# Mixture-of-experts output: weighted rows and an adding scatter in place of two rows per token and a combine

## The chip, the core and the metric

The kernel runs on one core of one Trainium2 chip. The core has TensorE (PE), VectorE (DVE), ScalarE (ACT), GpSimd (POOL) and SyncE (SP), each with its own instruction queue, and 16 DMA engines that all queues share. The metric is the device time of one execution in microseconds, lower is better.

## What is computed

The input x is 16 x 256 x 16 x 16 (batch, nodes, features, time). A spatio-temporal attention block with a Chebyshev graph convolution is added to x; then a group norm of the result goes through eight experts, of which each token uses two. A token is one of the 16 x 256 = 4,096 positions (batch, feature and time), with 256 channels. The change lies in the second part alone:

```
probs = softmax(x @ gate_w.T)                   # per token, 8 experts
rw, sel = top_k(probs, 2);  rw = rw / sum(rw)
combine = sum(one_hot(sel, 8) * rw)             # per token and expert
out = 0
for e in range(8):
    h = gelu(x @ w1[e].T) * (x @ w3[e].T)
    out = out + combine[:, e:e+1] * (h @ w2[e].T)
result = residual + transpose(out)              # back to channels first
```

## The kernel before

The work runs in stages: loads and attention statistics (to about 120 us of the profiled execution), the main phase over 16 batches with graph convolution, norms and routing (to about 435 us), the expert stage (444 to 671 us), and the last stage (671 to 717 us). The order on each engine is written out by hand, with semaphores between engines; there is no scheduler.

Routing (route_b and route_c on DVE) finds for each token its two experts, their weights r2[:, 3] / sum and r2[:, 4] / sum, and a slot for each in the DRAM tensor xrows, where the tokens of one expert stand together. POOL scatters the token's row there twice. A row is 256 channels and two numbers: the token's index (column N) and its first expert (column N + 1). Unused places of an expert's last tile are filled with rows whose index lies out of range.

The expert stage walks over RUN = 71 tiles of 128 rows. For each tile t, SP loads the rows (L312) into xt, of which there are four; PE transposes them (L605); DVE copies them out of PSUM (copy_x, L1400) and computes the row in yrows to which each result goes (L1403, L1406): the token's index, plus 4,096 if the tile's expert is not the token's first. PE does the first product (L618), ACT the gelu (L819), DVE the gate (L1411), PE a transposition (L626) and the second product (L633), with ACT's copy (L830) between these. ACT copies the result out of PSUM into one of four buffers yo (copy_y, L825), and POOL casts the destinations to integers (L936) and scatters 128 rows of 1 KB into yrows (put_rows, L940). So yrows has 8,192 rows, two for each token, each written once. POOL raises c_out, for which copy_y waits, after it has seen the scatter of three tiles earlier landed.

On PE the order within a tile is: transpose_rows of tile t + 3, down of t, turn_hidden of t + 1, up of t + 3.

The last stage goes over the 16 batches. SP loads both rows of each token (L332, L333; two transfers of 256 KB into one of four buffers yy), ACT multiplies the first with its weight (weigh_first, L854, two operations), DVE multiplies the second and adds (combine, L1435, two operations), PE transposes (L667, four), DVE adds the residual xs (L1444) into one of two buffers oo, and ACT issues the store (L859). These buffers, xt and yo among them, all lie over the tensor xT, which is the name that the profile shows.

Of the kernel before, what the change touches and what calls it, by code (L numbers as in the profile page):

```python
# [21 lines left out]
P = 128  # L22
# [13 lines left out]
ROW = N + 2  # L36
# [83 lines left out]
def build(nc, x, consts, small, cheb, vst, bst, w13t, w2t, xrows, yrows, out):  # L120
    with ExitStack() as ctx:
# [70 lines left out]
        wts = sb("wts", [B, 2, TT])  # L192
# [34 lines left out]
        dn = over_xT(2, 4, 1)  # L227
        used[0] = 0
        yy = over_xT(4, 2, TT, N)
        ym = over_xT(4, TT, N)  # L230
        ys = over_xT(2, TT, N)
        oo = over_xT(2, C, FT)
# [24 lines left out]
        d_ym = sem("d_ym"); c_ld = [sem(f"c_ld{i}") for i in range(SLOTS)]; c_tr = sem("c_tr"); c_xc = sem("c_xc"); c_up = sem("c_up")  # L257
# [4 lines left out]
        d_ld = [sem(f"d_ld{i}") for i in range(4)]; d_in = sem("d_in"); d_s = sem("d_s"); d_tr = sem("d_tr")  # L262
        d_o = sem("d_o"); d_st = [sem("d_st0"), sem("d_st1")]
# [8 lines left out]
        y_v = yrows[0:2 * TOKENS, :].rearrange("(w b k p) n -> p w b k n", w=2, b=B, k=TT)  # L272
# [10 lines left out]
        def _(sp):  # L283
# [16 lines left out]
            sp.wait_ge(fill_ready, 1)  # L300
            sp.dma_start(xrows[E * CAP:E * CAP + P, :], fill[:]).then_inc(fill_done, 16)
# [29 lines left out]
            def load_d(b, q):  # L331
                sp.dma_start(yy[:, q, 0], y_v[:, 0, b]).then_inc(d_ld[q], 16)  # L332
                sp.dma_start(yy[:, q, 1], y_v[:, 1, b]).then_inc(d_ld[q], 16)  # L333

            def landed(q, pairs):

                sp.wait_ge(d_ld[q], 32 * pairs)
                sp.sem_inc(d_in, 1)

            for q in range(4):  # L340
                load_d(q, q)
            landed(0, 1)
            landed(1, 1)
            with sp.Fori(0, B // 4 - 1) as i:
                for q in range(4):
                    landed((q + 2) % 4, i + (1 if q < 2 else 2))
                    sp.wait_ge(d_s, 4 * i + (q + 1 + START))
                    load_d(4 * i + (q + 4), q)
            landed(2, B // 4)
            landed(3, B // 4)  # L350
# [3 lines left out]
        def _(pe):  # L354
# [305 lines left out]
            with pe.Fori(0, B // 2) as i:  # L660
                for q in range(2):
                    b = 2 * i + q
                    pe.wait_ge(d_s, b + (1 + START))
                    pe.wait_ge(d_o, b + START - 1)
                    for c in range(C):
                        for k in range(TT):
                            last = nc.tensor.transpose(bank[6 + q][:, c * FT + k * P:c * FT + (k + 1) * P],  # L667
                                                       ys[:, q, k, c * P:(c + 1) * P], ident)
                    last.then_inc(d_tr, 1)
# [3 lines left out]
        def _(act):  # L673
# [148 lines left out]
            def copy_y(t, q):  # L822
                act.wait_ge(c_dn, t + (1 + START))
                act.wait_ge(c_out, t + 1)
                nc.scalar.copy(yo[:, t % 4], bank[4 + q][:, 0:N]).then_inc(c_y, 1)  # L825
# [23 lines left out]
            def weigh_first(b):  # L849
                act.wait_ge(d_in, b + 1)  # L850
                if not isinstance(b, int):
                    act.wait_ge(d_s, b + (START - 3))
                for k in range(TT):
                    ins = nc.scalar.mul(ym[:, b % 4, k], yy[:, b % 4, 0, k], wts[:, b, 0, k:k + 1])  # L854
                ins.then_inc(d_ym, 1)

            def store(b, q):
                act.wait_ge(d_o, b + (1 + START))
                act.dma_start(out_v[:, b], oo[:, q]).then_inc(d_st[q], 16)  # L859

            weigh_first(0)
            weigh_first(1)
            with act.Fori(0, B // 2 - 1) as i:
                for q in range(2):
                    weigh_first(2 * i + (q + 2))
                    store(2 * i + q, q)
            store(B - 2, 0)
            store(B - 1, 1)
            for q in range(2):
                act.wait_ge(d_st[q], 16 * (B // 2))  # L870
# [3 lines left out]
        def _(pool):  # L874
# [57 lines left out]
            def put_rows(t, q):  # L932

                pool.wait_ge(c_de, t + 1)
                pool.nop(nofuse=True)
                nc.gpsimd.tensor_copy(dest[:, q], dn[:, 1, q]).then_inc(c_di, 1)  # L936
                pool.wait_ge(c_y, t + (1 + START))
                pool.wait_ge(c_di, t + (1 + 4))
                pool.nop(nofuse=True)
                pool.indirect_dma_start(yrows, bass.IndirectOffsetOnAxis(ap=dest[:, q], axis=0),  # L940
                                        yo[:, q], None, bounds_check=2 * TOKENS - 1, oob_is_err=False
                                        ).then_inc(c_st[q], 16)

            for q in range(3):
                put_rows(q, q)
            with pool.Fori(0, (RUN - 3) // 4) as i:
                for q in range(4):
                    put_rows(4 * i + (q + 3), (q + 3) % 4)
# [7 lines left out]
        def _(dve):  # L956
# [296 lines left out]
            def route_b(b, p):  # L1253
# [22 lines left out]
                wb = wts[:, b]  # L1276
                V.tensor_tensor(wb[:, 0], r2[:, 3], r2[:, 8], ALU.mult)
                yield from step.then(V.tensor_tensor(wb[:, 1], r2[:, 4], r2[:, 8], ALU.mult))
# [248 lines left out]
```

## Time and profile before

| | us |
|---|---|
| median of 3 runs | 720.68 (719.37 to 721.49) |
| the profiled execution: its time | 719.21 |
| the profiled execution: its span, first to last instruction | 717.4 |
| expert stage, first to last scatter of results (71) | 458.0 to 668.4 |
| last stage, first load to the end | 670.7 to 717.4 |
| PE busy in the span, mean granted clock | 570.1, 0.883 |

The span is that of the instructions in one profiled execution; its time has 1.8 us around it. "Granted clock" is TensorE's clock as a share of 2.4 GHz; 0.50 is 1.2 GHz. A row of the timeline gives the start, the duration, and in brackets how long the engine was idle and what released it. A DMA issue counts on the engine that issues it; "to landing" is the time from the start of the issue until the data has arrived.

### The profile page before, as it was taken

What the parts mean: (1) busy time and instruction counts of PE and PEld (TensorE: products, weight loads), DVE (VectorE), ACT (ScalarE), POOL (GpSimd) and SP (SyncE); (2) the same over time, 40 slices, a digit from 0 to 9 for tenths busy, and PEclk for the clock granted to TensorE, in tenths of its full rate; (3) what the DMA queues carried; (4) which work ended last, traced back from release to release, by engine and by line L of the source; (5) the groups of instructions that cost most, each with busy time, mean ns of one, the idle gap of its engine ahead of it and who ended that gap; (6) DMA issues with size and microseconds to landing.
All of it is one profiled execution on the core that took longest, in us unless ns stands there. A gap on an engine that the chain in (4) does not pass through costs nothing. (4 is left out here: it accounts for less than half of the span.)

```text
span 717.4 us, 12846 instructions
## 1 busy us (share of the span) xinstructions
PE 570.1 (79%) x2508; PEld 372.1 (52%) x2509; DVE 426.7 (59%) x1891; ACT 250.4 (35%) x623; POOL 207.0 (29%) x265
## 2 busy tenths in 40 slices
PE   0566649999999999999997332999999999999344
PEld 0333325776666666666675110566666666666122
DVE  6755432687898888888888764333333333333255
ACT  0312214444444444444442210233333333333232
POOL 1000000111444444343444432133333333434100
PEclk9866668999999999999999655999999999999555
DMA  8910000000000000000000015122222222221497
GB/s 269 374 58 0 0 1 0 1 1 0 31 31 30 29 29 29 29 29 29 29 30 30 30 59 125 61 82 88 81 83 88 83 87 84 85 86 48 145 314 244
DMA packets 36247, 52.69 MB, mean 73 GB/s; under 512 B 4605, under 2 KB 31360, under 8 KB 35968
## 3 DMA queue, kind: packets, MB, share of 16 engines
q1 hardware_dynamic: 24816, 30.86, 13.7%
q0 software_dynamic: 6480, 16.85, 6.4%
q10 hardware_dynamic: 4928, 4.72, 2.0%
q8 instruction: 8, 0.13, 0.1%
q14 instruction: 15, 0.12, 0.1%
HBM read 30.19 MB, written 23.14 MB: 74 GB/s over the span
## 5 line engine op out<-in xcount | busy, mean ns | idle before, releaser
L618 PE MATMUL bank<-w,xT 128*128 x284 | 135.8, 601 | 2.1 <-DVE xT L1400 2.1
L1400 DVE COPY xT<-bank 128x256 f32<-128x256 f32 x71 | 30.2, 425 | 144.1 <-PE bank L605 144.1
L940 POOL DMA_INDIRECT yrows<-xT,dest x71 | 69.4, 977 | 140.5 <-ACT xT L825 136.3
L496 PE MATMUL bank<-work 128*128 128x256 f32 x384 | 94.8, 390 | 0.0
L909 POOL DMA_INDIRECT xrows<-xtok,slot x64 | 64.2, 1003 | 82.3 <-DVEq L1296 67.7
L897 POOL TENSOR_TENSOR yg<-work,sml 128x512 f32<-128x512 f32 x16 | 17.9, 1120 | 224.5 <-DVE work L1206 224.5
L496 PEld LDWEIGHTS bank<-work 128*128 128x128 f32 x384 | 71.5, 193 | 9.4 <-issue 0.8
L633 PE MATMUL bank<-w,xT 128*128 x284 | 74.2, 384 | 1.8 <-ACT xT L830 1.8
L618 PEld LDWEIGHTS bank<-w,xT 128*128 128x128 f32 x284 | 48.8, 192 | 37.6 <-issue 37.6
L819 ACT ACTIVATE xT<-bank 128x256 f32<-128x256 f32 x71 | 27.2, 383 | 95.3 <-PE bank L618 95.3
L633 PEld LDWEIGHTS bank<-w,xT 128*128 128x128 f32 x284 | 49.0, 192 | 6.5 <-issue 2.7
L825 ACT COPY xT<-bank 128x256 f32 (+1 forms) x71 | 26.4, 372 | 60.9 <-PE bank L633 60.9
L605 PEld LDWEIGHTS bank<-cst,xT 128*128 128x128 f32 x142 | 20.2, 143 | 52.7 <-issue 37.5
L487 PE MATMUL bank<-thetabd,xTb 128*128 128x384 f32 x128 | 46.6, 487 | 0.0
L773 ACT ACTIVATE xn<-xs,gr 128x256 f32 (+1 forms) x32 | 17.5, 592 | 71.1 <-DVE gr L1233 71.1
L667 PE MATMUL bank<-cst,xT 128*128 128x128 f32 x64 | 17.8, 433 | 29.1 <-DVE xT L1435 29.1
L605 PE MATMUL bank<-cst,xT 128*128 128x128 f32 x142 | 27.7, 277 | 15.1 <-DMA xT<-xrows 15.1
L467 PE MATMUL bank<-sg,vs 128*128 128x256 f32 x128 | 33.4, 406 | 2.5 <-ACT sg L735 1.4
L1155 DVE TENSOR_TENSOR work<-bank,chebs 128x768 f32<-128x768 f32 x32 | 30.1, 947 | 5.1 <-PE bank L478 5.1
L1411 DVE TENSOR_TENSOR xT<-bank,xT 128x256 f32<-128x256 f32 x71 | 30.2, 425 | 2.1 <-ACT xT L819 2.1
L755 ACT COPY work<-bank 128x384 f32<-128x384 f32 x64 | 28.9, 472 | 7.2 <-PE bank L487 6.5
L532 PE MATMUL bank<-xn,sml 128*8 128x256 f32 x64 | 19.0, 426 | 14.4 <-ACT xn L773 14.4
(204 smaller groups left out, 1060.6 us busy)
## 6 DMA issues: line engine op xcount, KB each, us to landing
xT<-xrows SPq DMA_DIRECT2D x71, 129.0 KB, 2.1
xT<-yrows SPq DMA_DIRECT2D x32, 256.0 KB, 4.0
xs<-x_in SPq DMA_DIRECT2D x4, 1024.0 KB, 6.6
w<-w13t_in SPq DMA_DIRECT2D x1, 4096.0 KB, 15.4
out<-xT ACTq DMA_DIRECT2D x16, 256.0 KB, 3.8
w<-w2t_in SPq DMA_DIRECT2D x1, 2048.0 KB, 19.8
yrows<-xT,dest POOLq DMA_INDIRECT x71, 2.4
xrows<-xtok,slot POOLq DMA_INDIRECT x64, 2.6
```

The source lines that it names most:

```text
L467: last = mm(bank[1][:, c * N:(c + 1) * N], vs[:, j, c * P:(c + 1) * P], sg[:, p, j], start=(j == 0), stop=(j == C - 1))
L487: mm(bank[4 + h][:, 0:K * P], xTb[:, p, h, c * P:(c + 1) * P], thetabd[:].rearrange("p k t o -> p (k t o)"), start=True, stop=True).then_i ...
L496: last = mm(bank[6][:, h * N:(h + 1) * N], z[:, p, c, k, h], A[:, p, c, k], start=(c == 0 and k == 0), stop=(c == C - 1 and k == K - 1))
L605: last = nc.tensor.transpose(bank[k % 2][:, c * P:(c + 1) * P], xt[:, k % SLOTS, c * P:(c + 1) * P], ident)
L618: last = mm(bank[2 + q][:, :], xc[:, q, c], w13[:, e, c].rearrange("p w n -> p (w n)"), start=(c == 0), stop=(c == C - 1))
L633: last = mm(bank[4 + q][:, 0:N], hT[:, q, f], w2[:, e, f], start=(f == 0), stop=(f == C - 1))
L755: nc.scalar.copy(z[:, p, c, :, h], bank[4 + h][:, 0:K * P].rearrange("p (k o) -> p k o", k=K)).then_inc(s["b_zc"], 1)
L909: pool.indirect_dma_start(xrows, bass.IndirectOffsetOnAxis(ap=slot[:, q, w, k:k + 1], axis=0), xtok[:, q, k], None).then_inc(sc_done[q], 16)
L940: pool.indirect_dma_start(yrows, bass.IndirectOffsetOnAxis(ap=dest[:, q], axis=0), yo[:, q], None, bounds_check=2 * TOKENS - 1, oob_is_err ...
L1155: ins = V.tensor_tensor(A[:, p, c], p3, chebs[:, c], ALU.mult)
L1400: V.tensor_copy(xc[:, q].rearrange("p c k -> p (c k)"), bank[q][:, 0:C * P]).then_inc(c_xc, 1)
L1411: V.tensor_tensor(hh[:, q].rearrange("p f k -> p (f k)"), bank[2 + q][:, C * P:2 * C * P], gl[:, q].rearrange("p f k -> p (f k)"), ALU.mul ...
```

## The change

The kernel gives each row four extra numbers in place of two: the two weights go with it (columns N + 2 and N + 3), so xrows has rows of 260 numbers. In the expert stage DVE computes the row's weight for the tile's expert as the sum of two products with a comparison (four operations where two stood), and copy_y multiplies with it while it copies. The destination is the token's index itself. yrows holds one row per token; the scatter adds to it, in DRAM. Since two scatters may add to one row, each waits until the one before it has landed. SP zeroes yrows ahead of that, with 16 transfers behind the weights' load, and POOL waits for them before the first scatter. In the last stage SP loads one row per token, six batches ahead; weigh_first and combine are gone, PE transposes straight from yy, and there are three buffers oo. The loops of that stage are written out in place of loops on the engines.

```diff
--- before.py
+++ after.py
@@ -33,7 +33,7 @@
 TT = FT // P
 TOKENS = B * FT
 CAP = TOKENS + P
-ROW = N + 2
+ROW = N + 4
 TILES = 2 * TOKENS // P + E
 EPS = 1e-5
 BITS = E.bit_length() - 1
...
@@ -224,12 +223,10 @@
         hh = over_xT(2, C, P)
         hT = over_xT(2, C, P)
         yo = over_xT(4, N)
-        dn = over_xT(2, 4, 1)
+        dn = over_xT(4, 4, 1)
         used[0] = 0
-        yy = over_xT(4, 2, TT, N)
-        ym = over_xT(4, TT, N)
-        ys = over_xT(2, TT, N)
-        oo = over_xT(2, C, FT)
+        yy = over_xT(6, TT, N)
+        oo = over_xT(3, C, FT)
 
 
         ld_c = sem("ld_c"); ld_w = sem("ld_w"); ld_m = sem("ld_m")
...
@@ -269,7 +266,7 @@
 
         x_v = x.rearrange("b (c p) f t -> p b c (f t)", p=P)
         out_v = out.rearrange("b (c p) f t -> p b c (f t)", p=P)
-        y_v = yrows[0:2 * TOKENS, :].rearrange("(w b k p) n -> p w b k n", w=2, b=B, k=TT)
+        y_v = yrows[0:TOKENS, :].rearrange("(b k p) n -> p b k n", b=B, k=TT)
 
         def fill_behind(eng, experts):
             for e in experts:
@@ -298,6 +295,9 @@
                 sp.dma_start(dst[:], src).then_inc(ld_m, 16)
 
             sp.wait_ge(fill_ready, 1)
+            zeros = fill[:, 0:N].rearrange("p (u n) -> p u n", u=1).to_broadcast([P, TT, N])
+            for b in range(B):
+                sp.dma_start(y_v[:, b], zeros).then_inc(z_done, 16)
             sp.dma_start(xrows[E * CAP:E * CAP + P, :], fill[:]).then_inc(fill_done, 16)
             sp.wait_ge(fill_rows, 1)
             fill_behind(sp, range(E // 2))
@@ -328,26 +328,14 @@
 
             for q in range(4):
                 sp.wait_ge(c_st[q], 16 * ((RUN + 3 - q) // 4))
-            def load_d(b, q):
-                sp.dma_start(yy[:, q, 0], y_v[:, 0, b]).then_inc(d_ld[q], 16)
-                sp.dma_start(yy[:, q, 1], y_v[:, 1, b]).then_inc(d_ld[q], 16)
-
-            def landed(q, pairs):
-
-                sp.wait_ge(d_ld[q], 32 * pairs)
-                sp.sem_inc(d_in, 1)
-
-            for q in range(4):
-                load_d(q, q)
-            landed(0, 1)
-            landed(1, 1)
-            with sp.Fori(0, B // 4 - 1) as i:
-                for q in range(4):
-                    landed((q + 2) % 4, i + (1 if q < 2 else 2))
-                    sp.wait_ge(d_s, 4 * i + (q + 1 + START))
-                    load_d(4 * i + (q + 4), q)
-            landed(2, B // 4)
-            landed(3, B // 4)
+            def load_d(b):
+
+                if b >= 6:
+                    sp.wait_ge(d_tr, b - 5)
+                sp.dma_start(yy[:, b % 6], y_v[:, b]).then_inc(d_ld[b % 6], 16)
+
+            for b in range(B):
+                load_d(b)
 
 
         @block.tensor
@@ -657,16 +645,15 @@
                     turn_hidden(t + 1, (t + 1) % 2)
 
 
-            with pe.Fori(0, B // 2) as i:
-                for q in range(2):
-                    b = 2 * i + q
-                    pe.wait_ge(d_s, b + (1 + START))
-                    pe.wait_ge(d_o, b + START - 1)
-                    for c in range(C):
-                        for k in range(TT):
-                            last = nc.tensor.transpose(bank[6 + q][:, c * FT + k * P:c * FT + (k + 1) * P],
-                                                       ys[:, q, k, c * P:(c + 1) * P], ident)
-                    last.then_inc(d_tr, 1)
+            for b in range(B):
+                pe.wait_ge(d_ld[b % 6], 16 * (b // 6 + 1))
+                if b >= 2:
+                    pe.wait_ge(d_o, b - 1)
+                for c in range(C):
+                    for k in range(TT):
+                        last = nc.tensor.transpose(bank[6 + b % 2][:, c * FT + k * P:c * FT + (k + 1) * P],
+                                                   yy[:, b % 6, k, c * P:(c + 1) * P], ident)
+                last.then_inc(d_tr, 1)
 
 
         @block.scalar
@@ -822,7 +809,8 @@
             def copy_y(t, q):
                 act.wait_ge(c_dn, t + (1 + START))
                 act.wait_ge(c_out, t + 1)
-                nc.scalar.copy(yo[:, t % 4], bank[4 + q][:, 0:N]).then_inc(c_y, 1)
+                act.wait_ge(c_de, t + 1)
+                nc.scalar.mul(yo[:, t % 4], bank[4 + q][:, 0:N], dn[:, 3, t % 4]).then_inc(c_y, 1)
 
             def copy_hidden(t, q):
                 act.wait_ge(c_ht, t + (1 + START))
@@ -846,28 +834,11 @@
             copy_y(RUN - 1, (RUN - 1) % 2)
 
 
-            def weigh_first(b):
-                act.wait_ge(d_in, b + 1)
-                if not isinstance(b, int):
-                    act.wait_ge(d_s, b + (START - 3))
-                for k in range(TT):
-                    ins = nc.scalar.mul(ym[:, b % 4, k], yy[:, b % 4, 0, k], wts[:, b, 0, k:k + 1])
-                ins.then_inc(d_ym, 1)
-
-            def store(b, q):
-                act.wait_ge(d_o, b + (1 + START))
-                act.dma_start(out_v[:, b], oo[:, q]).then_inc(d_st[q], 16)
-
-            weigh_first(0)
-            weigh_first(1)
-            with act.Fori(0, B // 2 - 1) as i:
-                for q in range(2):
-                    weigh_first(2 * i + (q + 2))
-                    store(2 * i + q, q)
-            store(B - 2, 0)
-            store(B - 1, 1)
-            for q in range(2):
-                act.wait_ge(d_st[q], 16 * (B // 2))
+            for b in range(B):
+                act.wait_ge(d_o, b + 1)
+                act.dma_start(out_v[:, b], oo[:, b % 3]).then_inc(d_st[b % 3], 16)
+            for q in range(3):
+                act.wait_ge(d_st[q], 16 * ((B + 2 - q) // 3))
 
 
         @block.gpsimd
@@ -929,23 +900,27 @@
 
             pool.sem_inc(c_di, 4)
 
-            def put_rows(t, q):
+            def put_rows(t, q, landed):
 
                 pool.wait_ge(c_de, t + 1)
                 pool.nop(nofuse=True)
                 nc.gpsimd.tensor_copy(dest[:, q], dn[:, 1, q]).then_inc(c_di, 1)
                 pool.wait_ge(c_y, t + (1 + START))
                 pool.wait_ge(c_di, t + (1 + 4))
+
+                if landed is not None:
+                    pool.wait_ge(c_st[(q - 1) % 4], landed)
                 pool.nop(nofuse=True)
                 pool.indirect_dma_start(yrows, bass.IndirectOffsetOnAxis(ap=dest[:, q], axis=0),
-                                        yo[:, q], None, bounds_check=2 * TOKENS - 1, oob_is_err=False
-                                        ).then_inc(c_st[q], 16)
-
+                                        yo[:, q], None, bounds_check=TOKENS - 1, oob_is_err=False,
+                                        compute_op=ALU.add).then_inc(c_st[q], 16)
+
+            pool.wait_ge(z_done, 16 * B)
             for q in range(3):
-                put_rows(q, q)
+                put_rows(q, q, 16 if q else None)
             with pool.Fori(0, (RUN - 3) // 4) as i:
                 for q in range(4):
-                    put_rows(4 * i + (q + 3), (q + 3) % 4)
+                    put_rows(4 * i + (q + 3), (q + 3) % 4, 16 * i + 16 * ((q + 2) // 4 + 1))
                     pool.wait_ge(c_st[q], 16 * (i + 1))
                     pool.sem_inc(c_out, 1)
             for q in range(4):
@@ -1273,9 +1248,8 @@
                 V.tensor_scalar(xtok[:, p, :, N + 1], r2[:, 5], -1.0, float(E), ALU.mult, ALU.add)
                 yield from step.then(V.tensor_tensor(r2[:, 7], r2[:, 3], r2[:, 4], ALU.add))
                 yield from step.then(V.reciprocal(r2[:, 8], r2[:, 7]))
-                wb = wts[:, b]
-                V.tensor_tensor(wb[:, 0], r2[:, 3], r2[:, 8], ALU.mult)
-                yield from step.then(V.tensor_tensor(wb[:, 1], r2[:, 4], r2[:, 8], ALU.mult))
+                V.tensor_tensor(xtok[:, p, :, N + 2], r2[:, 3], r2[:, 8], ALU.mult)
+                yield from step.then(V.tensor_tensor(xtok[:, p, :, N + 3], r2[:, 4], r2[:, 8], ALU.mult))
                 step.close()
 
             def route_c(b, p):
@@ -1400,10 +1374,14 @@
                 V.tensor_copy(xc[:, q].rearrange("p c k -> p (c k)"), bank[q][:, 0:C * P]).then_inc(c_xc, 1)
 
                 dve.wait_ge(c_di, t + 1)
-                V.tensor_scalar(dn[:, 0, m], xt[:, m, N + 1:N + 2], tb3[:, 0, bass.ds(t, 1)], float(TOKENS),
-                                ALU.not_equal, ALU.mult).then_inc(c_dd, 1)
+                if not isinstance(t, int) or t >= 4:
+                    dve.wait_ge(c_y, t + START - 3)
+                e = tb3[:, 0, bass.ds(t, 1)]
+                V.tensor_scalar(dn[:, 0, m], xt[:, m, N + 1:N + 2], e, xt[:, m, N + 2:N + 3], ALU.is_equal, ALU.mult)
+                V.tensor_scalar(dn[:, 2, m], xt[:, m, N + 1:N + 2], e, xt[:, m, N + 3:N + 4], ALU.not_equal, ALU.mult)
+                V.tensor_copy(dn[:, 1, m], xt[:, m, N:N + 1]).then_inc(c_dd, 1)
                 dve.wait_ge(c_dd, t + 1)
-                V.tensor_tensor(dn[:, 1, m], dn[:, 0, m], xt[:, m, N:N + 1], ALU.add).then_inc(c_de, 1)
+                V.tensor_tensor(dn[:, 3, m], dn[:, 0, m], dn[:, 2, m], ALU.add).then_inc(c_de, 1)
 
             def gate(t, q):
                 dve.wait_ge(c_gl, t + 1)
@@ -1424,37 +1402,12 @@
             gate(RUN - 1, (RUN - 1) % 2)
 
 
-            dve.sem_inc(d_o, START)
-            dve.sem_inc(d_s, START)
-
-            def combine(b, q):
-
-                dve.wait_ge(d_in, b + 1)
-                dve.wait_ge(d_ym, b + 1)
-                for k in range(TT):
-                    ins = V.scalar_tensor_tensor(out=ys[:, q, k], in0=yy[:, b % 4, 1, k], scalar=wts[:, b, 1, k:k + 1],
-                                                 in1=ym[:, b % 4, k], op0=ALU.mult, op1=ALU.add)
-                ins.then_inc(d_s, 1)
-
-            def residual(b, q, stored):
-
+            for b in range(B):
                 dve.wait_ge(d_tr, b + 1)
-                if stored is not None:
-                    dve.wait_ge(d_st[q], stored)
-                V.tensor_tensor(oo[:, q].rearrange("p c n -> p (c n)"), bank[6 + q][:, :],
+                if b >= 3:
+                    dve.wait_ge(d_st[b % 3], 16 * (b // 3))
+                V.tensor_tensor(oo[:, b % 3].rearrange("p c n -> p (c n)"), bank[6 + b % 2][:, :],
                                 xs[:, b].rearrange("p c n -> p (c n)"), ALU.add).then_inc(d_o, 1)
-
-            combine(0, 0)
-            for b in range(2):
-                combine(b + 1, 1 - b)
-                residual(b, b, None)
-            with dve.Fori(0, B // 2 - 2) as i:
-                for q in range(2):
-                    combine(2 * i + (q + 3), 1 - q)
-                    residual(2 * i + (q + 2), q, 16 * (i + 1))
-            combine(B - 1, 1)
-            residual(B - 2, 0, 16 * (B // 2 - 1))
-            residual(B - 1, 1, 16 * (B // 2 - 1))
 
 
 def constants():
```

On POOL, one tile of the loop of the expert stage and the start of the next, before the change (CAST is the cast of destinations, the DMA is the scatter; line numbers are those of the kernel before):

```order
L936 CAST dest<-xT 128x1 [waits c_de]
L937 REGISTER_ALU
L938 REGISTER_ALU [waits c_y]
L940 DMA yrows<-xT,dest 8320x256 [waits c_di]
L949 ISA
L934 REGISTER_ALU [waits c_st0]
L936 CAST dest<-xT 128x1 [waits c_de]
```

The same place after the change (lines are those of the changed kernel):

```order
L907 CAST dest<-xT 128x1 [waits c_de]
L908 REGISTER_ALU
L909 REGISTER_ALU [waits c_y]
L912 ISA [waits c_di]
L914 DMA yrows<-xT,dest 8320x256 [waits c_st2]
L924 ISA
L905 REGISTER_ALU [waits c_st0]
L907 CAST dest<-xT 128x1 [waits c_de]
```

The scatter now has the wait for c_st2 in front of it, which is the landing of the scatter just before; the cast of the next tile stays behind the scatter, as it was.

On DVE, one tile of the loop of the expert stage before the change (copy_x, the destination, gate):

```order
L1400 COPY xT<-bank 128x256 [waits c_up,c_tr]
L1403 ISA [waits c_di]
L1403 TENSOR_SCALAR xT<-xT,tb 128x1
L1406 TENSOR_TENSOR xT<-xT 128x1 [waits c_dd]
L1411 TENSOR_TENSOR xT<-bank,xT 128x256 [waits c_ht,c_gl]
```

The same tile after the change:

```order
L1374 COPY xT<-bank 128x256 [waits c_up,c_tr]
L1380 ISA [waits c_y,c_di]
L1380 TENSOR_SCALAR xT<-xT,tb 128x1
L1381 TENSOR_SCALAR xT<-xT,tb 128x1
L1382 COPY xT<-xT 128x1
L1384 TENSOR_TENSOR xT<-xT 128x1 [waits c_dd]
L1389 TENSOR_TENSOR xT<-bank,xT 128x256 [waits c_ht,c_gl]
```

Two small operations more stand between copy_x and gate, and the first of them also waits for c_y, ACT's copy_y of four tiles before.

## Rows read from the trace of the kernel before

**Rows 1.** Page, table 1: busy us (share of the span) and instructions of TensorE
```profile
...
PE 570.1 (79%) x2508; PEld 372.1 (52%) x2509; DVE 426.7 (59%) x1891; ACT 250.4 (35%) x623; POOL 207.0 (29%) x265
...
```

**Rows 2.** Windows: before the main phase, steady expert stage, last stage
```profile
core 0: us, PE busy (x) PEld busy (x) DVE busy (x) ACT busy (x) POOL busy (x), PEclk, DMA share, GB/s
40.00:60.00 20.00, 12.86 (x50) 6.48 (x50) 11.79 (x50) 4.42 (x9) 0.00 (x0) 0.67 0.00 0
465.00:620.00 155.00, 155.00 (x618) 95.72 (x617) 54.28 (x208) 52.69 (x154) 59.99 (x103) 1.00 0.27 85
671.00:717.40 46.40, 17.78 (x64) 11.44 (x64) 24.14 (x48) 14.52 (x32) 0.00 (x0) 0.50 0.84 271
...
```

**Rows 3.** Timeline, one tile: start us, us, engine line op tiles [idle before <-releaser]
```profile
...
540.23 0.42 DVE L1400 COPY xT<-bank 128x256 f32<-128x256 f32 x1 [1.94 <-PE bank L605]
...
540.57 0.20 DVE L1403 TENSOR_SCALAR xT<-xT,tb 128x1 f32<-128x1 f32 x1
...
540.80 0.16 DVE L1406 TENSOR_TENSOR xT<-xT 128x1 f32<-128x1 f32 x1
540.88 0.42 DVE L1411 TENSOR_TENSOR xT<-bank,xT 128x256 f32<-128x256 f32 x1
...
541.11 1.88 PE L618 MATMUL bank<-w,xT 128*128 x4
541.29 0.37 ACT L825 COPY xT<-bank 128x256 f32 x1 [0.83 <-PE bank L633]
...
542.58 0.98 POOL L940 DMA_INDIRECT yrows<-xT,dest  x1 [1.92 <-ACT xT L825]
...
```

**Rows 4.** Tile dest: duration ns, starts of the scatters, and time to landing
```profile
...
L940 POOL DMA_INDIRECT yrows<-xT,dest x71: 976/976/1002, 458.0 to 668.4; - x71
...
DMA to landing us min/median/max: 2.1/2.4/2.8
```

**Rows 5.** Timeline, scatters of routed rows of one batch in the main phase
```profile
...
308.62 0.17 DVE L1293 CAST slot<-slotf 128x4 int32<-128x4 f32 x1
...
309.66 1.01 POOL L909 DMA_INDIRECT xrows<-xtok,slot  x1 [4.36 <-DVEq L1296]
310.97 0.96 POOL L909 DMA_INDIRECT xrows<-xtok,slot  x1 [0.30 <-issue]
...
```

**Rows 6.** DMA, 465 to 620 us: queue share; issues with us to landing
```profile
...
q0 software_dynamic: 2490, 6.49, 10.4%
...
xT<-xrows SPq DMA_DIRECT2D x51, 129.0 KB, 2.1
...
```

**Rows 7.** Timeline: last scatter, first load of the last stage, last residual
```profile
...
668.43 0.98 POOL L940 DMA_INDIRECT yrows<-xT,dest  x1 [2.06 <-ACT xT L825]
670.67 0.40 SPq L332 DMA_DIRECT2D xT<-yrows  x1
...
714.04 0.69 DVE L1444 TENSOR_TENSOR xT<-bank,xs 128x512 f32<-128x512 f32 x1 [0.68 <-PE bank L667]
```

**Rows 8.** Chain that ended last, in order of time, in the last stage
```profile
...
679.47 4.68 DMA out<-xT
...
685.16 4.50 DMA out<-xT
...
```

**Rows 9.** DMA, 671 to 717.4 us
```profile
...
DMA packets 13057, 12.59 MB, mean 271 GB/s; under 512 B 768, under 2 KB 13056, under 8 KB 13056
...
xT<-yrows SPq DMA_DIRECT2D x32, 256.0 KB, 4.0
out<-xT ACTq DMA_DIRECT2D x16, 256.0 KB, 3.8
```

**Rows 10.** Timeline: the first tile's product L618
```profile
...
445.37 3.77 PE L618 MATMUL bank<-w,xT 128*128 x4 [0.70 <-DVE xT L1400]
...
```

**Rows 11.** Timeline of SP: its last issues ahead of 432 us
```profile
...
20.00 0.53 SPq L298 DMA_DIRECT2D w<-w2t_in  x1
20.57 0.43 SPq L301 DMA_DIRECT2D xrows<-fill  x1
...
```

More of the change, by code:

```diff
@@ L191, in build @@
         r2 = sb("r2", [10, TT])
-        wts = sb("wts", [B, 2, TT])
         cnt = sb("cnt", [E])
@@ L255, in build @@
         v_tb = sem("v_tb"); tables = sem("tables"); fill_rows = sem("fill_rows"); fill_ready = sem("fill_ready"); fill_done = sem("fill_done")
-        d_ym = sem("d_ym"); c_ld = [sem(f"c_ld{i}") for i in range(SLOTS)]; c_tr = sem("c_tr"); c_xc = sem("c_xc"); c_up = sem("c_up")
+        z_done = sem("z_done"); c_ld = [sem(f"c_ld{i}") for i in range(SLOTS)]; c_tr = sem("c_tr"); c_xc = sem("c_xc"); c_up = sem("c_up")
         c_gl = sem("c_gl"); c_h = sem("c_h"); c_ht = sem("c_ht"); c_hc = sem("c_hc"); c_dn = sem("c_dn"); c_y = sem("c_y"); c_dd = sem("c_dd")
@@ L260, in build @@
         c_st = [sem(f"c_st{i}") for i in range(4)]; c_out = sem("c_out")
-        d_ld = [sem(f"d_ld{i}") for i in range(4)]; d_in = sem("d_in"); d_s = sem("d_s"); d_tr = sem("d_tr")
-        d_o = sem("d_o"); d_st = [sem("d_st0"), sem("d_st1")]
+        d_ld = [sem(f"d_ld{i}") for i in range(6)]; d_tr = sem("d_tr")
+        d_o = sem("d_o"); d_st = [sem(f"d_st{i}") for i in range(3)]
         cs = lambda a, n: cst[:, a:a + n]
```

## The prediction

> **What bounds the kernel now.** I read the page first: TensorE is busy 570.1 of 717.4 us, 79% of the span [rows 1]. That share is an average, so I cut the span by stages. From 465 to 620 us, the steady part of the expert stage, PE is busy in all of 155.00 us at a granted clock of 1.00, while DVE has 54, ACT 53 and POOL 60 us; the 16 DMA engines are 27% busy. In the last stage, from 671 to 717.4 us, the shares turn round: PE 17.8 of 46.4 us, DMA 84% busy [rows 2]. So there are two stages here that the change touches, one set by PE and one by DMA.
>
> The pace of the expert stage is best read from its last engine. The 71 scatters of result rows (L940) start between 458.0 and 668.4 us [rows 4], so one tile takes 210.4 / 70 = 3.006 us. I then followed one tile through the engines: copy_x, two small DVE operations, gate, the first product (L618), copy_y, and the scatter [rows 3]. The point to see is the distance from copy_y to the scatter: the copy ends at 541.29 + 0.37 = 541.66 us and the scatter starts at 542.58, although POOL was idle for 1.92 us and nothing else was missing. The 16 groups of routing scatters show this too: the slots are written at 308.79 us, the first scatter starts at 309.66 (0.87 later), and the next, which waits for nothing, 1.31 after that, 0.30 after the end of the first [rows 5]. So 0.9 us pass between the release of a scatter and its start as recorded. They hide behind a preceding scatter only if the next may be released before that one is done. In the kernel before nobody waits for this: four result buffers give each scatter several tiles of time.
>
> **The added wait.** A scatter now waits until its predecessor has landed. On POOL it stands directly ahead of the DMA; the cast for the same tile stands ahead of the wait, but the cast of the next tile is queued behind the scatter. What follows is a ring of steps, none of which can overlap: release, 0.92 us to the start, landing, release of the next. Landing is 2.4 us from the start in the median (2.1 at the least, 2.8 at most) [rows 4], which already has the 0.98 us of descriptor writing in it. The signal itself is quick: the last scatter starts at 668.43 and SP issues the load that waits for it at 670.67, 2.24 later [rows 7]. A ring of plain scatters so takes 0.92 + 2.4 = 3.32 us, 0.31 more than the 3.006 us that PE leaves it. Over 70 intervals that is +22 us before the addition itself costs anything. PE and ACT follow: copy_y of tile t waits for c_out, which POOL raises only after it has issued the scatter of tile t-1, so the banks of the second product come free at the ring's pace.
>
> **The addition.** No row shows an adding scatter. Below, its surcharge on the landing is 0: it writes the same bytes with the same descriptors' targets, and I see no reason for it to be faster than a plain one. Above, I take a whole load in sequence ahead of the write: a tile's 129 KB load lands 2.1 us after its issue [rows 6]. Between them: queue 0 spends 10.4% of 16 engines over 155 us on 51 scatters, 0.32 us for each scatter on each engine [rows 6]. Reading the destination as well makes that 0.64 (+0.3). Descriptors for a second read, if they are written at the rate of the others, add up to half of 0.98 us, part of it under the transfer (+0.3). I choose 0.6, nearer the lower end, since the rows of a scatter can be read ahead of each other. The ring is then 3.92 us, 0.914 above 3.006: 70 x 0.914 = +64 us.
>
> The Trainium skill (Collectives: The Full Stack, Part 3, "Why ReduceScatter is half of AllGather") says that an adding transfer is slower not for the addition but since it reads two sources, both through one ring. By that alone the surcharge would be the 0.3 us of doubled transfer, which is a rival below; no row here shows an addition.
>
> The wait can't be dropped for speed: two tiles of different experts hold the same token, and both would add to one row. The Trainium skill (DMA: Bandwidth & Descriptors, Rules for kernel authors) says so too: an accumulating DMA reads its destination and writes it later, and one that lands in between is lost. No run here shows it, and it changes no number.
>
> **The last stage.** Gone are 16 of 32 loads of 256 KB, ACT's weighing (2 operations) and DVE's combine (2 operations, L1435) for each batch. The chain there runs through stores: 679.47 to 685.16 us from one store to the next in the chain, which is two batches, since residual waits for the store before last out of two buffers; the stores in between land after 4.68 and 4.50 us [rows 8]. Now there are three buffers. Two estimates: (a) 12.59 MB took 84% of 46.4 us, 39 us of full engines, 323 GB/s [rows 2, 9]; 8.39 MB take 26.0, and with the 7.4 us that the engines were not full, 33.4 us. (b) By latency: a period of about 5.2 us over three buffers, 1.75 a batch, 15 x 1.75 = 26, after some 6 us to the first store and ahead of 2.7 us from the last residual's end (714.73) to the end [rows 7]: 35 us. The stage gives back 11 to 13 us; I take 13. PE needs 1.1 us a batch even at its present clock of 0.50 there (17.78 us for 16), and DVE 0.69, so neither replaces DMA.
>
> **What costs nothing.** The 16 stores of zeros (4.2 MB, 13 us at 323 GB/s) are issued on SP after the weights' load at 20.00 us. The only transfer issued behind them until 432 us is the store of fill, and the DMA share from 40 to 60 us is 0.00 [rows 2, 11]. Without that cover they would cost 13 us. On DVE a tile gets two operations more and one other kind: 0.20 + 0.16 become four of about 0.2, +0.4 us. DVE idles 1.94 us ahead of each copy_x, and gate's result of 541.30 us is wanted by PE for the next tile's turn, over 2 us later [rows 3]. DVE's new wait for c_y is for the copy of four tiles back. copy_y changes from a copy to a product with a column, at the same shape. Rows of 260 for 258 numbers add 0.8% to transfers that are hidden. The weights' writes into xtok replace as many into wts, and the scatter of those rows is behind the same semaphore.
>
> **Sum.** The profiled execution took 719.2 us around a span of 717.4. 719.2 + 22 (ring of plain scatters) + 42 (70 x 0.6, the addition) - 13 = 770.2 us. That execution stands 1.5 us below the median of the three runs shown, 720.68; I leave it at 770.
>
> **Rivals.**
> - *The ring is hidden.* If most of the 0.92 us is preparation that POOL's queue does before the wait is fulfilled, the ring is 2.4 to 3.0 us and PE's 3.006 stays the pace: 719.2 - 13 = 706. For it: 0.30 us between neighbouring scatters. Against it: at 309.66 and at 542.58 an idle POOL, its instruction waiting, still took 0.87 and 0.92. It is faster than before if the ring stays under 3.006 + 13/70 = 3.19 us. Chance 0.12.
> - *Only the reads double.* Surcharge 0 to 0.3: ring up to 3.62, 719.2 + 43 - 13 = 749, down to 728. For it: transfers are a small part of the landing. Chance 0.22.
> - *The addition is slow, or PE's clock falls.* Surcharge over 1.1: 70 x 1.42 - 13 + 719.2 = 805 and more; with a full load in sequence (ring 5.42) 875. At a ring of 3.92 PE is busy 77% of the time. Four L618 products took 3.77 us at the lower clock at the stage's start [rows 10] against 1.88 later; if half of the tiles ran so, at 6.0 us each, the mean would be 4.96 and the time 843. Chance 0.18.
> - My forecast, surcharge 0.3 to 1.1, 749 to 805 us: 0.44. A ring within 0.03 us of 3.19, where gain and loss meet: 0.04.
>
> **How the numbers follow.** A measurement here tells 0.3% (2.2 us) from no change. Faster is the first rival, 0.12; same 0.04; slower is the rest, 0.84. The range must take in the second rival's 728 and reach into the third; 722 to 838 leaves out the hidden ring (0.12) and the far end of the slow addition (0.07). The forecast's own range is 749 to 805.
>
> **What would show it.** In the profile after, the scatters' mean interval should be 3.9 us (3.3 if the addition is free), the wait ahead of the scatter should go from copy_y to the scatter before it, PE should show a gap of 0.9 us per tile, and landing should read 3.0 in place of 2.4. The last stage should take 33 us with no SCALAR_TENSOR_TENSOR in it. A mean interval of 3.0 proves the first step wrong; an interval of 3.3 the surcharge alone.

## The result: 814.4 us, 13% slower

The changed kernel takes 814.36 us (813.15 to 816.02, 4 runs) against 720.17 us before in the same job: a ratio of 1.129 [1.127, 1.132]. The forecast had slower at 0.84 and 770 us; the time lies in its range of 722 to 838, in the third rival's part of it, to which I had given 0.18; the central case, 749 to 805 us at 0.44, ends 9 us short of it. The profiled execution has a span of 812.6 us, 95.2 more than before.

**Pace of the expert stage.** The view of the scatters' destinations in the changed kernel, which answers to [rows 4]; the first two columns of a row are line and engine, then duration in ns (min/median/max) and first and last start:

```profile
L907 POOL CAST dest<-xT x71: 183/781/801, 446.4 to 777.6; 128x1 int32<-128x1 f32 x71
L914 POOL DMA_INDIRECT yrows<-xT,dest x71: 1557/1569/1629, 458.8 to 780.1; - x71
its engine sat idle before it (us, times) until:
  DMA yrows<-xT,dest: 183.9, 66
...
DMA to landing us min/median/max: 2.7/3.8/4.3
```

The interval is (780.1 - 458.8) / 70 = 4.590 us, where it was 3.006. POOL now waits for its own last transfer 66 times. Landing takes 3.8 us in place of 2.4, and POOL's own record of a scatter, which I take for the writing of its descriptors, 1.57 in place of 0.98.

One turn of the ring in the timeline, with PE and ACT behind it:

```profile
...
601.94 1.56 POOL L914 DMA_INDIRECT yrows<-xT,dest  x1 [2.94 <-DMA yrows<-xT,dest]
602.07 0.48 ACT L813 ACTIVATE xT<-bank,xT 128x256 f32 x1 [3.70 <-POOLq L925]
...
602.92 0.78 POOL L907 CAST dest<-xT 128x1 int32<-128x1 f32 x1
...
603.14 1.13 PE L621 MATMUL bank<-w,xT 128*128 x4 [1.45 <-issue]
...
606.46 1.57 POOL L914 DMA_INDIRECT yrows<-xT,dest  x1 [2.75 <-DMA yrows<-xT,dest]
```

The order of releases has turned round: in [rows 3] the scatter waited for copy_y; here copy_y (L813) waits 3.70 us for POOL to raise c_out (L925), and PE's second product (L621) starts 1.45 us late behind it. The bracket names no releaser for this one; over the span, the profile puts 61.0 of the 88.1 us that PE idles ahead of L621 down to ACT's L818, which stands behind copy_y on ACT.

**Windows**: the time of zeroing and the steady expert stage. These answer to [rows 2]:

```profile
core 0: us, PE busy (x) PEld busy (x) DVE busy (x) ACT busy (x) POOL busy (x), PEclk, DMA share, GB/s
40.00:60.00 20.00, 12.53 (x49) 6.46 (x50) 12.15 (x52) 3.86 (x8) 0.00 (x0) 0.59 0.56 196
500.00:700.00 200.00, 143.43 (x521) 82.70 (x520) 62.40 (x259) 45.16 (x132) 77.64 (x88) 0.99 0.36 56
...
```

PE is busy in 72% of the time from 500 to 700 us, at a clock of 0.99. (From 740 to 777 us, at the stage's end, the clock is 0.87, with PE busy in 24.0 of 37 us.) The zeros fill a window from 40 to 60 us that was empty.

**The DMA queue of the scatters** from 480 to 700 us (packets, MB, share of 16 engines), which answers to [rows 6]:

```profile
q0 software_dynamic: 6891, 5.95, 24.2%
```

48 scatters start in this window: 144 packets for one, and 0.242 x 220 / 48 = 1.11 us on each DMA engine. Before it was 49 packets and 0.32 us, for the same 0.12 MB.

**The last stage.** The last scatter, the loads behind it, and the first residual, answering to [rows 7]:

```profile
780.09 1.57 POOL L914 DMA_INDIRECT yrows<-xT,dest  x1 [1.75 <-DMA yrows<-xT,dest]
782.96 17.88 SPq L335 DMA_DIRECT2D xT<-yrows  x16
...
787.09 0.69 DVE L1409 TENSOR_TENSOR xT<-bank,xs 128x512 f32<-128x512 f32 x1 [22.03 <-PE bank L654]
...
793.41 0.69 DVE L1409 TENSOR_TENSOR xT<-bank,xs 128x512 f32<-128x512 f32 x1 [0.50 <-DMA out<-xT]
```

From the first load at 782.96 to 812.6 it is 29.6 us, where it was 46.7. From the fourth batch on, the first that needs a buffer again, the residual is held in 10 of 13 batches by a store (the bracket), though there are three buffers. The stage in the window's columns of above:

```profile
783.00:812.60 29.60, 16.74 (x64) 11.83 (x64) 11.05 (x16) 0.00 (x0) 0.00 (x0) 0.56 0.86 283
```

The span's 95.2 us are thus: 70 x (4.590 - 3.006) = +110.9 in the ring, +0.8 until the first scatter, +0.6 from the last one to the first load (2.87 for 2.24 us), -17.1 in the last stage.

### The profile page after: what moved, and what is told of

Read it like the earlier page. It is cut to its first block and busy times, and to the rows that moved or that the text cites. A ratio compares the mean times of both kernels' runs of the same rounds, so it can differ in the third digit from the quotient of the medians.

```text
span 812.6 us, 12753 instructions
## 1 busy us (share of the span) xinstructions
PE 592.2 (73%) x2508; PEld 377.6 (46%) x2509; DVE 441.1 (54%) x2001; ACT 237.0 (29%) x591; POOL 249.4 (31%) x265
## 5 line engine op out<-in xcount | busy, mean ns | idle before, releaser
L914 POOL DMA_INDIRECT yrows<-xT,dest x71 | 111.3, 1568 | 209.7 <-DMA yrows<-xT,dest 183.9
L621 PE MATMUL bank<-w,xT 128*128 x284 | 82.7, 415 | 88.1 <-ACT xT L818 61.0
L606 PE MATMUL bank<-w,xT 128*128 x284 | 138.6, 612 | 2.1 <-DVE xT L1374 2.1
L813 ACT ACTIVATE xT<-bank,xT 128x256 f32 (+1 forms) x71 | 33.8, 476 | 242.7 <-POOLq L925 119.9
L621 PEld LDWEIGHTS bank<-w,xT 128*128 128x128 f32 x284 | 49.7, 195 | 107.6 <-issue 103.6
L1374 DVE COPY xT<-bank 128x256 f32<-128x256 f32 x71 | 30.1, 425 | 114.9 <-PE bank L593 114.9
L1380 DVE TENSOR_SCALAR xT<-xT,tb 128x1 f32<-128x1 f32 x71 | 19.3, 272 | 102.6 <-POOL dest L907 102.6
L606 PEld LDWEIGHTS bank<-w,xT 128*128 128x128 f32 x284 | 50.4, 198 | 39.3 <-issue 39.3
L907 POOL CAST dest<-xT 128x1 int32<-128x1 f32 x71 | 54.8, 772 | 7.3 <-DVE xT L1384 7.3
L593 PE MATMUL bank<-cst,xT 128*128 128x128 f32 x142 | 27.7, 277 | 13.4 <-DMA xT<-xrows 13.4
L1130 DVE TENSOR_TENSOR work<-bank,chebs 128x768 f32<-128x768 f32 x32 | 30.1, 947 | 5.1 <-PE bank L466 5.0
L1389 DVE TENSOR_TENSOR xT<-bank,xT 128x256 f32<-128x256 f32 x71 | 30.1, 425 | 2.9 <-ACT xT L806 2.9
```

The lines of the kernel that those rows point to most:

```text
L593: last = nc.tensor.transpose(bank[k % 2][:, c * P:(c + 1) * P], xt[:, k % SLOTS, c * P:(c + 1) * P], ident)
L606: last = mm(bank[2 + q][:, :], xc[:, q, c], w13[:, e, c].rearrange("p w n -> p (w n)"), start=(c == 0), stop=(c == C - 1))
L621: last = mm(bank[4 + q][:, 0:N], hT[:, q, f], w2[:, e, f], start=(f == 0), stop=(f == C - 1))
L813: nc.scalar.mul(yo[:, t % 4], bank[4 + q][:, 0:N], dn[:, 3, t % 4]).then_inc(c_y, 1)
L1130: ins = V.tensor_tensor(A[:, p, c], p3, chebs[:, c], ALU.mult)
L1374: V.tensor_copy(xc[:, q].rearrange("p c k -> p (c k)"), bank[q][:, 0:C * P]).then_inc(c_xc, 1)
```

## The experiments

My theory: the time is lost in a ring (release, start, landing) that nothing overlaps, and the addition lengthens the landing. The rivals: the wait alone is harmless; adding scatters are a bound in throughput; something else in the changed tile, such as the weighted copy or DVE's operations, sets the pace.

**1. The wait alone.** The kernel before with the wait added:

```diff
                 pool.wait_ge(c_di, t + (1 + 4))
+                if landed is not None:
+                    pool.wait_ge(c_st[(q - 1) % 4], landed)
                 pool.nop(nofuse=True)
...
```

> The kernel before with one thing added: each scatter waits until its predecessor has landed. Scatters stay plain, two rows per token. My theory (a ring of release, start, landing): release to start 0.8 us (as the adding scatters of the changed kernel show it) plus 2.4 us landing gives 3.2 us per filled tile against 3.006, 67 filled tiles: +13 us, about 732 us; with 0.92 us as in the prediction 3.32 and +21, 740 us. Rival (the addition is the whole loss, the wait alone is hidden behind PE): 720 us, interval 3.01.

Measured: 735.36 us against 718.65, ratio 1.025 [1.022, 1.028]. Its scatters, in the same view:

```profile
L942 POOL DMA_INDIRECT yrows<-xT,dest x71: 976/979/1003, 456.7 to 682.8; - x71
...
DMA to landing us min/median/max: 2.1/2.4/2.7
```

The interval is 226.1 / 70 = 3.230 us. A ring of plain scatters is longer than PE's work by 0.22 us: 2.4 of landing and 0.83 from release to start. The rival of a harmless wait is out. Of the 16.7 us measured, 70 x 0.224 = 15.7 are the ring's.

**2. The changed kernel with a plain scatter**, still one at a time:

```diff
-                                        yo[:, q], None, bounds_check=TOKENS - 1, oob_is_err=False,
-                                        compute_op=ALU.add).then_inc(c_st[q], 16)
+                                        yo[:, q], None, bounds_check=TOKENS - 1, oob_is_err=False
+                                        ).then_inc(c_st[q], 16)
```

> The changed kernel with a plain scatter in place of the adding one (this leaves out the sum of the two experts of a token, the later one overwrites); the wait stays. Ring theory: interval 3.2 us as in the run with the wait alone, last stage 29.6 us as in the changed kernel, so 719 + 13 - 17 = 715 us, descriptor writing back at 0.98 us and landing at 2.4. Rival (something else in the changed expert stage, such as the weighted copy or the four DVE operations, holds the pace): interval stays near 4.6, 814 us.

Measured: 720.56 us, ratio 1.003 [1.001, 1.004] (ten runs from 717.8 to 723.9):

```profile
L914 POOL DMA_INDIRECT yrows<-xT,dest x71: 977/979/1002, 458.6 to 690.3; - x71
```

The interval is 231.7 / 70 = 3.31, and descriptor writing is back at 0.98 us. The rival of 4.6 is out: POOL waits for its own last transfer here too (68 times), and not for the weighted copy or DVE's four operations. Taking one argument of one instruction away gives back some 92 us (94.2 above the kernel before in one job, 1.9 in the other). The expectation of 715 us was missed by 5.6, for the interval is 0.08 above run 1: landing is 2.5 in the stage's middle for 2.4, and two scatters land only after 3.3 and 4.0 us. What makes the plain landing longer in the changed kernel stays open.

**3. Adding without the wait**, each tile to rows of its own (not shown: 16 further transfers of zeros for the second half of yrows, and the bound of 2 * TOKENS - 1):

```diff
-                if landed is not None:
-                    pool.wait_ge(c_st[(q - 1) % 4], landed)
...
-                V.tensor_copy(dn[:, 1, m], xt[:, m, N:N + 1]).then_inc(c_dd, 1)
+                V.tensor_scalar(dn[:, 1, m], xt[:, m, N + 1:N + 2], e, float(TOKENS), ALU.not_equal, ALU.mult).then_inc(c_dd, 1)
...
+                V.tensor_tensor(dn[:, 1, m], dn[:, 1, m], xt[:, m, N:N + 1], ALU.add).then_inc(c_de, 1)
```

> Adding scatters without the wait: each tile adds to rows of its own (8192 rows, all zeroed, 32 zero stores), and the last stage still loads one row per token (this leaves out the second expert's part). Latency theory: the addition costs only where it is waited for, POOL needs 1.57 + 0.3 us per scatter and DMA 1.1 us per engine, both under PE's 3.006: interval 3.01, 719 - 17 = 702 us. Rival (the adding scatter is a bound in throughput, on POOL or the DMA engines): interval over 3.2, over 715 us.

Measured: 702.22 us, ratio 0.978 [0.975, 0.981]. The timeline shows a scatter released by the copy again, as 62 of the 71 are:

```profile
559.78 1.56 POOL L915 DMA_INDIRECT yrows<-xT,dest  x1 [1.12 <-ACT xT L816]
```

and in the view of destinations:

```profile
L915 POOL DMA_INDIRECT yrows<-xT,dest x71: 1557/1569/1629, 460.2 to 670.3; - x71
```

First to last start is 210.1 us, interval 3.00. The addition is no bound in throughput at this pace: it costs its latency, and only where that is waited for. The 16.4 us gained are the one-row last stage (30.1 us from its first load to the end).

**4. No rows in the adding scatter**: every destination out of range.

```diff
-                V.tensor_copy(dn[:, 1, m], xt[:, m, N:N + 1]).then_inc(c_dd, 1)
+                V.tensor_scalar(dn[:, 1, m], xt[:, m, N:N + 1], float(TOKENS), None, ALU.add).then_inc(c_dd, 1)
```

> The changed kernel with every destination out of range, so that no row is written (this leaves out the experts' whole result); adding form and wait stay. The last three scatters of the changed kernel, of tiles without tokens, came 3.5 us apart and landed in 2.7. Theory: the rows' transfer is 1.1 us of the ring, so all intervals become 3.5 us and the expert stage 70 x 1.07 = 75 us shorter, near 739 us. Rival (the last scatters are quicker for another reason, such as that the loads of tiles are over): interval 4.4 to 4.6.

Measured in one run: 744.8 us (739 expected), and

```profile
L914 POOL DMA_INDIRECT yrows<-xT,dest x71: 1557/1569/1629, 459.9 to 710.6; - x71
...
DMA to landing us min/median/max: 2.7/2.7/4.1
```

The interval is 3.58 us. So of the filled ring's 4.59, 1.0 is the rows' transfer. The plain scatter's empty tiles land in 2.1 (the least value in [rows 4]), its filled ones in 2.4. The addition's surcharge of 1.4 us on the landing has two parts: 0.6 is there without rows, as much as the writing of descriptors has grown, and 0.8 comes with the rows' transfer.

**5. Half the bytes**: the first 128 of 256 columns of each row (yh is yrows seen as rows of half the length, so the index is doubled).

```diff
-                pool.indirect_dma_start(yrows, bass.IndirectOffsetOnAxis(ap=dest[:, q], axis=0),
-                                        yo[:, q], None, bounds_check=TOKENS - 1, oob_is_err=False,
+                pool.indirect_dma_start(yh, bass.IndirectOffsetOnAxis(ap=dest[:, q], axis=0),
+                                        yo[:, q, 0:N // 2], None, bounds_check=2 * TOKENS - 1, oob_is_err=False,
...
-                V.tensor_copy(dn[:, 1, m], xt[:, m, N:N + 1]).then_inc(c_dd, 1)
+                V.tensor_scalar(dn[:, 1, m], xt[:, m, N:N + 1], 2.0, None, ALU.mult).then_inc(c_dd, 1)
```

> The changed kernel scattering the first 128 of 256 columns of each row alone (this leaves out half of the channels' sum), 512 bytes where 1 KB was; the number of rows and of descriptors is the same. The filled ring of 4.59 us has 1.1 us over the empty one of 3.58. If the transfer goes by bytes the interval becomes 4.1 us, 779 us in all; if by rows it stays at 4.5 to 4.6, 812 us.

Measured in one run: 780.4 us:

```profile
L916 POOL DMA_INDIRECT yrows<-xT,dest x71: 1557/1569/1630, 459.2 to 746.7; - x71
```

The interval is 4.11, landing 3.3. The part of the ring above the empty one goes by bytes: 0.53 us for 1.01, while the rows and their packets (143 for a scatter) are as many as before. The time on each DMA engine follows less closely: 0.173 x 220 / 54 = 0.70 us for 1.11.

**6. Two rings in turn**: even and odd tiles add to different halves of yrows, and each scatter waits for the one two tiles back (not shown: the zeros for both halves, and TOKENS added to the destination for odd tiles).

```diff
-                    pool.wait_ge(c_st[(q - 1) % 4], landed)
+                    pool.wait_ge(c_st[(q - 2) % 4], landed)
```

> The changed kernel with two halves of yrows: even tiles add to one, odd tiles to the other, and a scatter waits for the landing of the scatter two tiles back in place of the one before. The last stage loads the even half alone (this leaves out what the odd tiles added). Theory (the wait costs by latency, 4.59 us for one turn of the ring, now shared by two tiles, 2.3 each): PE's 3.01 us is the pace again, 702 us as in the run without waits. Rival (adding scatters that overlap slow each other, their 1.1 us on each DMA engine and 1.57 us on POOL in a row): interval 3.2 to 3.5, 716 to 737 us.

Measured: 703.64 us, ratio 0.977 [0.972, 0.982]:

```profile
L917 POOL DMA_INDIRECT yrows<-xT,dest x71: 1558/1569/1630, 459.5 to 670.0; - x71
```

The interval is 210.5 / 70 = 3.01, landing still 3.8. A ring of 4.6 us costs nothing if two tiles share it. A whole kernel would have to load both halves again in the last stage, which takes back what the adding scatter was for. There is a cheaper way that no run tried: the tiles come in the order of the experts, and a token's two experts differ, so two tiles of one expert never share a token. Only where the expert changes, at most seven times in 71 tiles, must a scatter wait for those before it. What such a kernel would take is not shown.

**7. Two rows per token, weighted in the copy**, plain scatters, no wait; in the last stage two loads and one addition on DVE for each batch, six pairs of row buffers and four result buffers.

```diff
-        yy = over_xT(6, TT, N)
-        oo = over_xT(3, C, FT)
+        yy = over_xT(6, 2, TT, N)
+        oo = over_xT(4, C, FT)
...
+                V.tensor_tensor(yy[:, b % 6, 0], yy[:, b % 6, 0], yy[:, b % 6, 1], ALU.add).then_inc(d_s, 1)
...
```

> The other half of the change without the adding scatter: rows weighted in copy_y, plain scatters to two rows per token with no wait, and a last stage as in the changed kernel but with two loads of 256 KB per batch, one DVE addition, six buffers for rows and four for results. Theory A (the last stage before was held by store latency over two buffers, DMA engines can move more): 12.59 MB at 350 to 380 GB/s is 33 to 36 us plus 6 of head and tail, 40 to 42 against 46.7 us, so 713 to 716 us (median of before 720). Theory B (DMA was full at 96%): 46 us, no change.

Measured: 710.48 us, ratio 0.987 [0.983, 0.991]; the last stage is 39.6 us in place of 46.7. Theory A held. Since this run changed the weighing and the build of the last stage at once, run 8 parts these two.

**8. The last stage rebuilt, the weighing kept**: the kernel before, unweighted rows, its own weighing in place on ACT and DVE, with the buffers of run 7. The loops are written out too, SP no longer waits for a load to land before it issues a later one, and a row buffer is loaded again once PE, and not DVE, has read it.

```diff
-        yy = over_xT(4, 2, TT, N)
-        ym = over_xT(4, TT, N)
-        ys = over_xT(2, TT, N)
-        oo = over_xT(2, C, FT)
+        yy = over_xT(6, 2, TT, N)
+        oo = over_xT(4, C, FT)
...
```

> The kernel before with the buffers and the written-out order of the two-row run in its last stage (six pairs of row buffers, four result buffers), but with its own weighing on ACT and DVE, in place. Theory A (the gain of that run came from the buffers, the stage being held by stores over two buffers): 40 us for the stage, 711 to 714 us in all, as with weighted rows. Theory B (it came from leaving out ACT's weighing and one of DVE's two operations): 46 us, 719 us.

Measured: 709.52 us, ratio 0.987 [0.983, 0.990], the same as run 7. Its last stage in the window's columns of above:

```profile
672.00:708.70 36.70, 17.85 (x64) 11.46 (x64) 23.85 (x48) 14.52 (x32) 0.00 (x0) 0.50 0.96 324
```

ACT does as much weighing as before and the gain is there all the same. This window starts 3.5 us after the stage's first load; over the whole stage, 668.5 to 708.7 us, the DMA engines are at 92% where they were at 84%. Weighting in the copy gives nothing by itself. Runs 7 and 8 can't be told apart; they are the fastest versions whose edits leave nothing of the output out, 1.3% below the kernel before. Which of the edits to the stage gives the 6.5 us (46.7 to 40.2), no run tells. For the result buffers speak the chain of stores in [rows 8] and run 9. But SP's waits for landings, behind which it issued the later loads in the kernel before (19.4 us in all), went as well, and they remain a rival.

**9. Six result buffers** in the changed kernel in place of three.

```diff
-        oo = over_xT(3, C, FT)
+        oo = over_xT(6, C, FT)
...
```

> The changed kernel with six result buffers in place of three in the last stage. The residual waits there for stores (out<-xT) in most batches. Theory (store latency, 3.7 us landing and 0.8 us of residual over three buffers, 1.5 us a batch): with six buffers the DMA engines are the bound, 8.39 MB at up to 380 GB/s, and the stage takes 26 to 28 us in place of 29.6. Rival (DMA is the bound already): 29.6 us as before.

Measured in one run: 810.1 us, and the last stage:

```profile
781.60:808.20 26.60, 15.78 (x64) 10.98 (x64) 11.06 (x16) 0.00 (x0) 0.00 (x0) 0.56 0.93 315
```

26.6 us, 3.0 less; of 9.9 us in which the residual waited for stores, one wait of 0.4 us is left. The result buffers are all that this edit changes, so stores did hold the changed kernel's last stage with three of them.

**10. The changed kernel again**, beside runs 5 and 8:

> The changed kernel once more, beside the other two on one chip: 814 us, interval of scatters 4.59 us, last stage 29.6 us.

Measured: 813.40 us, ratio 1.131 [1.126, 1.135]; scatters from 458.6 to 779.6 us, interval 4.59; from the first load at 782.46 to the span's end at 812.5 it is 30.0 us.

## Why the prediction was right in direction and 44 us short

**The added wait: right.** I had said that the ring of plain scatters takes 3.32 us and costs 22. Run 1 measured 3.230 and 15.7 us, run 2, in the changed kernel, 3.31 and 21.3. The second comes that close by luck: it has a longer landing (2.5) with a shorter start (0.8) than I had written. The step from release to start was 0.83 us, not 0.92; the landing was the 2.4 of [rows 4]. That POOL, ACT and PE follow the ring was as described.

**The addition: mis-sized.** This is the term that failed: 42 us (70 x 0.6) forecast, 70 x (4.590 - 3.230) = 95.2 measured against run 1, a surcharge of 1.36 on the ring; against the ring of run 2 it is 89.6 us, or 1.28. My two parts were 0.3 for descriptors and 0.3 for the transfer. I put the growth of descriptor writing at half of 0.98 us at most, and part of that under the transfer. It grew by 0.59 (0.98 to 1.57), and run 4 has as much in the landing (2.1 to 2.7). The transfer grew by 0.8 us (0.3 to 1.1), not by 0.3: each engine is busy 3.5 times as long for a scatter, not twice. Why it is that much, with three times the packets for the same bytes, stays open.

The Trainium skill (Collectives: The Full Stack, Part 3, "Why ReduceScatter is half of AllGather") gives the second read as the cost, a factor of about two. The trace disagrees in size: 0.32 to 1.11 us on each engine, 49 to 144 packets, so "only the reads double", 728 to 749 us, falls.

**The third rival: its first half.** "The addition is slow" was put at a surcharge over 1.1 and 805 us and more; that is what happened. "PE's clock falls" did not in the steady stage: 0.99 at 72% busy. "The ring is hidden" is out by run 1.

**The last stage: 13 forecast, 17.1 measured.** I took the bandwidth of the old stage, 323 GB/s, as that of the new one, and a store ring of 1.75 us a batch. The new stage does a batch in (809.27 - 787.09) / 15 = 1.48 us. Runs 8 and 9 say that the old stage was not held by the DMA engines alone: rebuilt, with two rows still, it takes 40 us, and the new one with six result buffers 26.6. Between these the halved loads are worth 13 to 14 us, as forecast. The whole is 6.5 (46.7 to 40.2) and 13.6 (40.2 to 26.6), less the 3.0 that three result buffers still held back: 17.1. How much of the 6.5 is owed to more buffers and how much to the order of waits, no run tells.

**Costs put at nothing: right.** The zeros went into the empty window. Run 2 holds the four DVE operations and the weighted copy and still has a plain ring's pace (3.31), and run 3 has them at PE's. The first scatter starts 0.8 us later than before; runs 1 and 8, which are the kernel before up to that point, start it at 456.7 and 457.0 us against 458.0, so a difference of that size is not clear of the spread.

**The sum again with the measured terms**: 719.2 + 15.7 + 95.2 - 17.1 + 0.8 + 0.6 = 814.4 us, the profiled execution's own time.

## What to carry to other kernels

A transfer that must wait for its predecessor is priced by its whole latency, from release through preparation to landing (4.59 us here), and set against the loop's pace (3.006); that it fits by throughput, as run 3 shows, says nothing about it. Two targets used in turn halve that price, but check first that this leaves the saving intact. Check also which predecessors can touch the same rows: here most could not. Where a stage looks full of DMA at 84%, ask what a store's buffer is waited for: here more buffers and an order with fewer waits gave 1.3% with no arithmetic changed.

## What I had not expected of the hardware

- An adding scatter of 128 rows of 1 KB into DRAM lands 3.8 us after its start; a plain one takes 2.4. With no row in range they take 2.7 and 2.1, with rows of 512 bytes the adding one takes 3.3.
- Adding scatters that don't wait for each other (run 3) keep the pace of 3.00 us, though each keeps the 16 engines busy for about 1.1 us.
- The cast behind an adding scatter is recorded with 0.78 us, not 0.20. It starts 0.98 us after the scatter's start, as it did before, and its record ends after that of the scatter. DVE waits for it ahead of L1380 (61 times, 102.6 us in all), but POOL idles only 7.3 us in all for DVE's results, so the ring doesn't pass through it.
- One scatter of a tile without tokens landed in 4.3 us (the one at 767.95), between filled ones at 3.8 and empty ones at 2.7. Plain scatters do it too: of the last four, one landed in 2.8 in the kernel before and one in 4.0 in run 2, the others in 2.1. It stays unexplained.
